# An audio tower on one core: coefficients, variances and head norms as rows spread by matmuls, expert gates spread by DMA, written-out orders for the whole run

## What is computed

```python
def _ssm_layer(x, A_log, Dp, W_dbc, W_dt, b_dt):
    A = -exp(A_log)
    delta, Bm, Cm = split(x @ W_dbc.T, [1, 1 + 64])          # one delta, 64 B, 64 C per token
    delta = softplus(delta @ W_dt.T + b_dt)
    hs = scan of h = exp(delta * A) * h + delta * x * Bm       # 64 states
    return sum over states of hs * Cm  + Dp * x
# three such layers; after the first two, pairs of steps are averaged (375 -> 187 -> 93)
h = tok(x)
h = h + attn(layernorm(h))     # q, k normalised per head of 8 channels; y divided by its own norm
h = h + moe(layernorm(h))      # router -> softmax -> top 2 of 6 experts; each 64-64-64-64 with relu
```

## Time and profile before

| | |
|---|---|
| median of 3 runs | 776.01 us (769.16 to 778.88) |
| the profiled execution, its own time | 778.98 us |
| its span in the trace | 777.2 us |
| mean granted TensorE clock | 0.952 |
| busy: PE, DVE, ACT, POOL | 87%, 79%, 67%, 43% |

### The profile page before, as it was taken

One profiled execution on the slowest core, in us unless ns is written; L12 is line 12 of the kernel. 1 busy time (PEld: TensorE's weight loads), 2 busy tenths in 40 slices (PEclk: granted clock), 3 DMA queues, 4 the chain that ended last, 5 costly groups with the idle time before them and its releaser, 6 DMA issues.

```text
span 777.2 us, 18707 instructions
## 1 busy us (share of the span) xinstructions
PE 677.7 (87%) x7686; PEld 317.6 (41%) x7686; DVE 617.4 (79%) x1082; ACT 524.6 (67%) x930; POOL 331.9 (43%) x291
## 2 busy tenths in 40 slices
PE   4766689899999999999999998999999997988774
PEld 2322234344444444444444453444444433433321
DVE  6899889789898989898989898987888986755230
ACT  1442476858788787878687968677786848575631
POOL 6455462636444646454645534353545252311000
PEclk9985899999999999999999999999999999999875
DMA  3332221112021211212030303111201001000001
GB/s 76 74 83 49 49 46 31 25 32 56 22 54 32 47 40 32 56 24 63 16 71 14 73 2 73 43 26 44 48 19 37 9 1 36 7 8 4 5 6 26
DMA packets 78694, 28.32 MB, mean 36 GB/s; under 512 B 70407, under 2 KB 78599, under 8 KB 78599
## 3 DMA queue, kind: packets, MB, share of 16 engines
q1 hardware_dynamic: 71904, 26.08, 14.7%
q10 hardware_dynamic: 6695, 0.95, 0.7%
HBM read 13.30 MB, written 3.05 MB: 21 GB/s over the span
## 4 chain that ended last, share of the span: by engine, by line
PE 65%; DVE 14%; ACT 11%; issue 4%; DMA 2%; SPq 2%; POOL 1%; DVEq 0%; ACTq 0%
PE ring L1004 19%; ACT pm L837 7%; PE ring L1074 6%; PE ring L1061 5%; PE ring L1160 4%; PE ring L1132 3%; PE ring L1011 3%; PE ring L1015 3%; PE ring L1036 3%; PE ring L1141 2%; PE ring L977 2%; PE ring L1123 2%; PE ring L1029 2%; PE ring L1098 2%; PE ring L1091 2%
## 5 line engine op out<-in xcount | busy, mean ns | idle before, releaser
L837 ACT ACTIVATE pm<-ring,two_col 93x744 f32<-93x744 f32 x128 | 105.8, 872 | 12.5 <-PE ring L1061 10.9
L1439 DVE TENSOR_TENSOR hidw<-hid,ring 128x744 f32<-128x744 f32 x48 | 44.4, 926 | 30.0 <-PE ring L1123 22.5
L1061 PE MATMUL ring<-q_exp,qk 32*93 32x372 f32 x512 | 56.4, 509 | 13.2 <-ACT pm L837 8.7
L1074 PE MATMUL ring<-pm,v 97*32 97x93 f32 x2048 | 53.5, 250 | 9.5 <-ACT pm L837 8.8
L693 POOL TENSOR_TENSOR h_in<-base_D,carry_D 128x372 f32<-128x372 f32 x16 | 17.0, 1061 | 102.2 <-DVE base_D L1327 102.2
L689 POOL TENSOR_TENSOR du_A<-delta_A,x_A 128x744 f32<-128x744 f32 x16 | 37.4, 2339 | 50.4 <-ACT delta_A L785 38.9
L872 ACT ACTIVATE hid<-ring,b_col 128x372 f32<-128x372 f32 x96 | 49.1, 563 | 8.2 <-PE ring L1141 8.2
L1074 PEld LDWEIGHTS ring<-pm,v 97*32 97x32 f32 x2048 | 42.3, 112 | 27.6 <-ACT pm L837 19.2
L711 POOL TENSOR_TENSOR q_exp<-qk,mask_q 128x1488 f32<-128x1488 f32 x16 | 42.9, 2682 | 17.6 <-DVE qk L1377 17.4
L879 ACT ACTIVATE hid<-ring,b_col 128x744 f32<-128x744 f32 x48 | 42.2, 878 | 12.0 <-PE ring L1132 7.9
L1132 PE MATMUL ring<-hid,w 64*64 64x372 f32 x384 | 42.8, 517 | 5.8 <-ACT v L829 3.4
(11 more groups left out here) (280 smaller groups left out, 1819.6 us busy)
## 6 DMA issues: line engine op xcount, KB each, us to landing
xin_A<-in_x_dram SPq DMA_DIRECT2D x62, 93.0 KB
xin_B<-in_x_dram SPq DMA_DIRECT2D x62, 93.0 KB
x_A<-x_A SPq DMA_DIRECT2D x32, 93.0 KB, 2.4
x_B<-x_B SPq DMA_DIRECT2D x32, 93.0 KB, 2.2
x_C<-x_C SPq DMA_DIRECT2D x32, 93.0 KB, 2.7
out_dram<-osb SPq DMA_DIRECT2D x15, 186.0 KB
x_D<-x_D SPq DMA_DIRECT2D x32, 46.5 KB, 1.9
w<-in_L_ffn_expert_w_dram SPq DMA_DIRECT2D x6, 48.0 KB
```

Source lines behind the costliest of these rows:

```text
L837: a.activation(pm[q % 2][h][0:TOUT].rearrange("m a j n -> m a (j n)"), out_of(f"att.s{q}{h}")[0:TOUT, :, 0:COLS], ACT.Square, bias=two_col ...
L1061: ins = mm(o[h][0:TOUT, b, 0:COLS], qk[r:r + 32, 1, q * TOUT:(q + 1) * TOUT], q_exp[r:r + 32, q].rearrange("p j n -> p (j n)"), start=True ...
L1074: ins = mm(o[32 * j:32 * j + 32, 0, h * TOUT:h * TOUT + TOUT], rows[:, at:at + 32], pm[q % 2][h][:, b, j, :], start=(b == 0), stop=(b == 1 ...
L1439: tt(hidw[k][:], hid2[:], out_of(f"ffn.g_{k}")[:, :, 0:COLS], ALU.mult).then_inc(me, 1)
```

## The change

- **Rows.** A new PE job `row` multiplies x with three weight columns into a few rows (128x32 weights, half or quarter of the columns), ACT copies them out (`rows`), and `dpre`, `b`, `c` become products of one-hot 64x64 blocks of ones (`row_back`) with these rows: eight matmuls of half the columns in place of four. W_dt becomes the scale of ACT's Exp. `alive` and the accumulators go; DVE takes the maximum of the rows instead (`most`), and at the end a few small steps make the flag.
- **Norms.** `cen` runs as four 64x64 blocks of 186 columns, `var` as four 128x32 ones of 93, ACT's Ln and Exp work on 93 columns in place of 372, and a new job `rs` spreads the result. The mean is taken out of the weights beforehand.
- **Head norms.** ACT evicts q and k with bias (`qkb`), squares them from SBUF, `n2` makes rows, clamp, Ln and Exp work on 186 columns, a new job `nq` spreads them, `hat` is one product. ACT copies v in place of DVE.
- **Gates.** The split, the selection matmuls and `hid2` go. PE transposes the gates in f32 to 6 partitions, ACT copies them, and a new step of SP, `gates`, copies each expert's partition to 64 partitions by DMA. `hidw` is one DVE operation, max(h2, -b2) times gate; what that leaves out is added to b3 beforehand.
- **Orders.** Every engine's list is written out for all 16 groups, and each PE job has a bank number of its own.

```diff
@@ SyncE @@
+                if s == "gates":
+                    need(g, "act ffn.gateT")
+                    need(g, *(f"dve ffn.hidw{k}" for k in range(NEP)), back=1)
+                    for e in range(NX):
+                        half = slice(E * (e % 2), E * (e % 2) + E)
+                        sp.dma_start(gate_all[half, e // 2].rearrange("p h c -> p (h c)"),
+                                     gateT[e:e + 1].rearrange("e h c -> e (h c)")[:, None, :].broadcast_to([1, E, 2 * COLS])).then_inc(done["sp ffn.gates"], 16)
@@ ScalarE @@
+                if s == "row":
...
+                    a.activation(rows[u][:], out_of(f"{u}.row", g)[:, 0, 0:WIDE[u] // 2], ACT.Copy).then_inc(me, 1)
...
-                    a.activation(rstd[w][:], rstd[w][:], ACT.Exp, scale=-0.5).then_inc(me, 1)
+                    a.activation(ln_rows[w][:], ln_rows[w][:], ACT.Exp, scale=-0.5).then_inc(me, 1)
...
+                        ins = a.activation(halves(qk_raw[:, b]), qk_made(b, g), ACT.Identity, bias=bqk_col[:, b:b + 1])
+                    ins.then_inc(me, 1)
+                if s == "qksq":
+                    need(g, "act att.qkb")
+                    need(g, "pe att.n2", back=1)
+                    a.activation(qk_sq[:], qk_raw[:], ACT.Square).then_inc(me, 1)
...
-                if s[:4] == "hid2":
...
-                    a.activation(hid2[:], out_of(f"ffn.h2_{k}")[:, :, 0:COLS], ACT.Relu, bias=b2_col[:, k:k + 1]).then_inc(me, 1)
...
+                    a.activation(gateT[:], out_of("ffn.gT", g)[0:NX, :, 0:COLS], ACT.Copy).then_inc(me, 1)
@@ TensorE @@
+                elif s == "row":
...
+                            ins = mm(o[to:to + 32, 0, 0:chunk], row_w[:, l].rearrange("p h r -> p (h r)"),
+                                     xs[u][:, b, h * chunk:(h + 1) * chunk], start=True, stop=True, tile_position=(0, to))
+                    ins.then_inc(me, 1)
+                elif s in ("dpre", "b", "c"):
+                    need(g, f"act {u}.row")
...
+                                ins = mm(o[to:to + E, b, h * chunk:(h + 1) * chunk], row_back[s][r:r + E, h, to:to + E],
+                                         rows[u][r:r + E, :], start=True, stop=True, tile_position=(r, to))
...
-                    mm(o[:, 0, 0:COLS], blk_mean[:], rstd[u[0]][:], start=True, stop=True).then_inc(me, 1)
+                    for q in range(NPAIR):
+                        ins = mm(o[32 * q:32 * q + 32, 0, 0:TOUT], ln_sum[:], cen_sq[u[0]][:, q * TOUT:(q + 1) * TOUT],
+                                 start=True, stop=True, tile_position=(0, 32 * q))
...
-                if s[:2] == "g_":
...
-                        ins = mm(o[:, h, 0:COLS], sel[:, h, k], gateT[:], start=True, stop=True)
...
+                            ins = nc.tensor.transpose(o[0:NX, h, q * TOUT:(q + 1) * TOUT], gate[:, 2 * q + h, :],
+                                                      ident[0:TOUT, 0:TOUT])
@@ VectorE @@
-                if s == "alive":
-                    need(g, f"act {u}.ln")
-                    v.tensor_reduce(seen[:, 0, FLAG[u], g:g + 1], delta[u][:], AX_X, ALU.min).then_inc(me, 1)
+                if s == "most":
+                    need(g, f"act {u}.row")
+                    v.tensor_reduce(seen[:, FLAG[u], g % NG:g % NG + 1], rows[u][:], AX_X, ALU.max).then_inc(me, 1)
...
-                    need(g, f"pe ffn.g_{k}", f"act ffn.hid2_{k}")
+                    need(g, f"pe ffn.h2_{k}", "sp ffn.gates")
                     need(g, "pe ffn.o", back=1)
-                    tt(hidw[k][:], hid2[:], out_of(f"ffn.g_{k}")[:, :, 0:COLS], ALU.mult).then_inc(me, 1)
+                    stt(hidw[k][:], out_of(f"ffn.h2_{k}", g)[:, :, 0:COLS], b2_neg[:, k:k + 1], gate_all[:, k],
+                        ALU.max, ALU.mult).then_inc(me, 1)
```

Of the orders the diff shows little:

```diff
-            "sp": ("D.swap:3 A.load:0 C.swap:2 B.load:0 ffn.store:7 A.swap:0 B.swap:0"),
...
+            "sp": ("prep.l1:0 prep.l4:0 prep.l0:0 A.load:0 A.load:1 A.swap:0 B.load:0 B.load:1 B.swap:0 A.load:2 "
...
+                    "D.swap:7 A.load:10 C.swap:8 ffn.gates:5 ffn.store:4 A.swap:9 B.load:11 B.swap:10 ffn.store:5 "
```

More of the change, by code:

```diff
@@ L96, in audio_tower @@
         m_quad = sb("m_quad", [P, LAYERS, P])
-        m_delta = sb("m_delta", [P, LAYERS, P])
-        m_b0 = sb("m_b0", [P, LAYERS, P])
-        m_c0 = sb("m_c0", [P, LAYERS, P])
+        row_w = sb("row_w", [P, LAYERS, 2, 16])
+        row_in = sb("row_in", [P, 16])
+        row_back = {j: sb(f"row_back_{j}", [P, 2, P]) for j in ("dpre", "b", "c")}
+        wdt_col = sb("wdt_col", [P, LAYERS])
+        nwdt_col = sb("nwdt_col", [P, LAYERS])
+        ones_row = sb("ones_row", [4, P])
+        most = sb("most", [P, 4])
+        most_of = sb("most_of", [4, 2])
+        most_at = sb("most_at", [4, 2, 4])
+        ends = sb("ends", [P, 2, 4])
+        least = sb("least", [P, 4])
         decay = sb("decay", [P, LAYERS, NS])
@@ L125, in audio_tower @@
         b2_col = sb("b2_col", [P, NEP])
[L126 to L127 removed]
+        b2_neg = sb("b2_neg", [P, NEP])
+        b2_at = sb("b2_at", [P, NEP, NX])
+        b3_row = sb("b3_row", [NX, E])
         def per_unit(name, extra=0):
@@ L141, in audio_tower @@
         carry = per_unit("carry")
-        base = per_unit("base")
-        seen = sb("seen", [P, 2, 4, NG])
+        base = quad
+        seen = sb("seen", [P, 4, NG])
+        rows = {u: sb(f"rows_{u}", [P, WIDE[u] // 2]) for u in UNITS}
         gen_w = sb("gen_w", [P, 2, P])
@@ L436, in audio_tower @@
         FFN_STEPS = NORM_STEPS + ["pe rh", "act rh", "pe lg", "dve route1", "act prexp", "dve top",
-                                  "act topexp", "dve gate", "pool split", "pe gT", "act gateT"]
+                                  "act topexp", "dve gate", "pe gT", "act gateT", "sp gates"]
         for k_ in range(NEP):
-            FFN_STEPS += [f"pe h1_{k_}", f"act hid1_{k_}", f"pe h2_{k_}", f"act hid2_{k_}", f"pe g_{k_}", f"dve hidw{k_}"]
+            FFN_STEPS += [f"pe h1_{k_}", f"act hid1_{k_}", f"pe h2_{k_}", f"dve hidw{k_}"]
         FFN_STEPS += ["pe o", "dve fin", "pe oT", "act out", "sp store"]
@@ L485, in audio_tower @@
         done = {who: sem(f"{who.replace(' ', '_').replace('.', '_')}_done") for who in
-                ("pe", "act", "dve", "pool", "sp A.load", "sp B.load", *(f"sp {u}.swap" for u in UNITS), "sp ffn.store")}
+                ("pe", "act", "dve", "pool", "sp A.load", "sp B.load", *(f"sp {u}.swap" for u in UNITS), "sp ffn.store", "sp ffn.gates")}
+        BANK = {(w, g): b for w, b in SPARE.items() for g in range(NG, 2 * NG)}
+        for entry in ORDER["pe"].split():
+            step_, banks_ = entry.split("/")
+            w_, g_ = step_.split(":")
+            BANK |= {(job, int(g_)): int(b) for job, b in zip(PAIRED.get(w_, (w_,)), banks_.split(","))}
         BEFORE = {}
@@ L902, in prepare @@
             def prepare(g, u, s):
+                if s == "ends":
+                    q = sem("ends_exp")
+                    need(g, "dve prep.ends")
+                    a.activation(least[:], least[:], ACT.Exp).then_inc(q, 1)
+                    act.wait_ge(q, 1)
+                    a.activation(least[:], least[:], ACT.Ln, bias=1.0).then_inc(me, 1)
                 for k in range(2):
@@ L945, in bank @@
                     need(g_e, *JOBS[earlier][1:])
-                return out_of(job)
+                return out_of(job, g)
             def prepare(g, u, s):
                 o = bank(g, f"prep.{s}")[:, 0]
+                if s == "most":
+                    need(g, "dve prep.most")
+                    nc.tensor.transpose(o[0:4, 0:P], most[:], ident[:]).then_inc(me, 1)
+                if s == "ends":
+                    need(g, "dve prep.mostof")
+                    mm(o[:, 0:8], ones_row[:], most_at[:].rearrange("p k u -> p (k u)"), start=True, stop=True).then_inc(me, 1)
                 if s == "flag":
@@ L1154, in experts @@
                     o = bank(g, "ffn.o")
-                    for i in range(3):
-                        mm(o[:, 0, 0:COLS], b3_part[i][:].rearrange("r h e -> r (h e)"), gateT[:],
-                           start=(i == 0), stop=(i == 2))
+                    for h in range(2):
+                        mm(o[E * h:E * h + E, 0, 0:COLS], b3_row[:], gateT[:, h], start=True, stop=False,
+                           skip_group_check=True, tile_position=(0, E * h))
                     for k in range(NEP):
@@ new lines, in prepare @@
+                if s == "ends":
+                    need(g, "pe prep.ends")
+                    found = out_of("prep.ends", g)[:, 0, 0:8].rearrange("p (k u) -> p k u", k=2)
+                    for u, l in UNITS.items():
+                        for k, w in enumerate((wdt_col, nwdt_col)):
+                            ts(ends[:, k, FLAG[u]:FLAG[u] + 1], found[:, k, FLAG[u]:FLAG[u] + 1], w[:, l:l + 1], bdt_col[:, l:l + 1],
+                               ALU.mult, ALU.add).then_inc(c, 1)
+                    dve.wait_ge(c, 8)
```

(7 more changed lines are left out.)

481 lines of the change are left out of this document (280 added, 201 removed), and 513 rows, old and new, of tables (FIRST, LAST, ORDER).

## The result

The changed kernel takes 1,379.2 us (median of 4 runs, 1,377.0 to 1,383.0), the kernel before 772.6 (767.2 to 778.9): a ratio of 1.790, 95% interval 1.776 to 1.804. It is slower by 607 us. The forecast was 1,250, and its own range, 930 to 1,400, holds the result; of the cases, the time is nearest to rival (c), 1,400.

A forecast was written before the change was run, and what follows sets the result against it. One source partition limits the gate DMAs, so DVE waits at `hidw`: 151 us to the first gate, 15 intervals of 68.8 (1,032), 44 for the last gates, 24 to the end: 1,251, about 1,250 us; own range 930 to 1,400, 8-in-10 range 740 to 1,400.

The forecast's parts named there:

- rival (c): Worse than forecast: PE at its lower clock in the stalls, swaps behind the gates late too; 1,400 us, chance 0.07.
- The gates' price: Six broadcast DMAs per group, each from one partition to 64, between `gate` and `hidw`: 41 us with landing.
- two engines' worth: Rate assumed for reading one source partition in the gate DMAs: 28.6 GB/s, 39 us before landing.
- us to landing of gate_all near 40: Sign in the changed kernel's profile: the gate DMAs' landing time on tile gate_all, near 40 us.
- DVE stands about 33 us per group: DVE, in order, waits at `hidw` for all six gate DMAs: about 33 us per group.
- The rows between: DVE's work before the next `gate` can come, priced by durations: 9 to 41 us per interval, mean 24.8.
- busy time within 15 us of before: Sign said to hold in either case: PE's busy time stays within 15 us of the kernel before.
- the one path: The path from `gate` to `hidw`, on which the prediction turns: intervals of 68.8 us in place of 39.9.
- Swap landings of tens of us: Sign on SP's queue: swaps stand behind the gate DMAs and take tens of us to land.
- The gains without the gates: Savings from the other parts: DVE 47 us, ACT 40 us, PE 0.65 us a group, start 10 us.
- case without the loss: Rival in which the broadcast is spread well and PE bounds again: 747 us, range 735 to 762, chance 0.25.
- rival (d): The new orders themselves lose a wait a group: 15 to 30 us; no chance given for it alone.

The follow-up runs named there:

- e12: Changed kernel with the six narrow gate DMAs issued from GpSimd's queue and `hidw` reading a constant tile without waiting for them: 1,257.4 us, ratio 1.617.
- e2: Changed kernel without the gate DMAs and the waits for them, gate_all holding the constant 0.25 from the start: 784.8 us, ratio 1.021.
- e7: Changed kernel, whole computation, with the gate written 16 times so that each gate DMA reads 16 partitions instead of one: 818.6 us, ratio 1.062.
- e6: Changed kernel with its narrow gate DMAs issued as before, but `hidw` reading a constant tile without waiting for them: 1,264.1 us, ratio 1.643.
- e11: Changed kernel, whole computation, `hidw` still waiting, with the six narrow gate DMAs moved from SyncE's queue to GpSimd's: 1,361.3 us, ratio 1.766.

## Why the prediction was right, and where not

**The gates' price: right, in size partly by luck.** The term "41 us with landing" measured 41.3 in the kernel and 41.8 alone. It stood on two engines' worth, 28.6 GB/s, chosen from a range of one to four (78 to 20 us); the choke gave 27 alone and 33 in e12 as a mean over the time in which its packets were held. No row before the change fixed that choice. The picture behind it was not quite what happened either: not two engines' streams pass, but sixteen engines are busy 86% of the time and move 27 GB/s together. The time of the six is the same by both, but only the second says that every other transfer is held as well. The sign "us to landing of gate_all near 40" did not come as written: one gate DMA lands in a median of 22.1 us, and 41 is the time of the six.

**DVE stands about 33 us per group: right.** 571.8 / 16 = 35.7 us. With the 3 us for transpose and copy, `gate` to `hidw` was summed as 44 and measured 45.8.

**The rows between, mis-sized.** The 24.8 us from `hidw` to the next `gate` measured 30.6. This is the largest term of the miss: 5.8 x 15 = 87 of the 127 us between 1,251 and the span of 1,378. It was priced from VectorE's durations alone, and its idle time was put at nothing. Summed in the trace, VectorE is busy 22.6 of the 30.6 us, 2.2 less than priced, and idle 8.0. In e2, where no gate DMA runs, it is busy the same 22.6 of 28.8 and idle 6.2: that much is VectorE's waiting for others in any case, and 1.8 us come with the gates. The rest of the miss: 1.8 x 15 = 27 in `gate` to `hidw`, 17 in the start, and 6 less at the end (62.4 against 68).

**Rival (c): both signs are there, but they explain little of the number.** The mean granted clock fell to 0.76 of full speed, between the levels of 1.2 and 2.4 GHz, and TensorE's busy time rose by 40 us over e2 with the same instructions; swaps landed late. The forecast of "busy time within 15 us of before" is wrong by that (33 more). But VectorE's path sets the interval, and from e7 to the changed kernel its part beside the gates grows by 1.3 us only (29.3 to 30.6). The time came out nearest to (c) for the reason above, not for (c)'s.

**What the prediction did not see** is that its wait was replaceable. It read the late swaps as a companion of the wait; e6 and e12 show that the same transfers hold the kernel at 1,260 with no wait at `hidw` at all. That this is also the forecast's number is chance, since the forecast got there by the wait. The steps of the sum held; its claim to be the one path did not.

**Swap landings of tens of us: half right.** Their median stays at 2.3 to 2.8 us; those that meet the gates take up to 14.8 us to land in the changed kernel, and the rest of their delay is that SyncE issues them late: at the wait of 38.8 us, the longest, 36.4 us lie before the issue of the swap.

**The gains without the gates: terms right, sum wrong.** `alive` went as said:

```profile
L1583 DVE TENSOR_REDUCE seen<-rows_A 128x1 f32<-128x186 f32 x16 | 5.4, 339 | 14.7 <-ACT rows_A L920 14.7
```

339 ns where it took 918, 32 us less over the units, and v's copy is gone. `hidw` cost 2 us, not 7. But `quad`'s three-operand steps cost 6 us more than `base`'s, and the router's rows up to `gate` 14 more, with no reason shown (8 and 12 in e2): VectorE has 30 us less in the changed kernel, not 47. ScalarE has 35 less, forecast 40. TensorE has 0.4 us a group less to do in e2 (6.6 us in all), forecast 0.65. For its case without the loss the prediction took 1.55 us off each interval; e2 shows 0.5. The start, forecast 10 us shorter, was 15 us longer. Together this turned 747 us into 785: 25 us in the start, 16 in the intervals, and 8 back at the end, which was to be 4 us longer and is 4 shorter (33 of the 38; the rest is the difference between a profiled execution and the median). By its kind this is rival (d), the orders, although the experiments do not show by which entries.

## What to carry to other kernels

Price a broadcast DMA at its narrower end: count the partitions that it reads as well as those that it writes, and if it reads one, write the row several times first (here 0.75 us of VectorE per group took 33.5 us off the way from `gate` to `hidw`). A slow transfer can cost more than its own wait: here every other transfer met the same engines, so before you hide the wait, ask what else needs a DMA in that time. And when one removal leaves the loss in place, remove two at once before you name the cause: here neither the wait nor the queue, nor both together, took away more than 122 of the 607 us, and the width of the source took away 561.

No version here beats the kernel before; the best with the whole computation is e7, at 1.062 of its time.

## What the runs showed of the hardware that was not expected

A gate DMA is issued in a median of 0.60 us in e7, and the first two of a group in 0.5 to 0.6 us in the changed kernel too, mostly; from the fourth on, with narrow ones ahead of it on SyncE's queue, it takes about 7 us. From GpSimd's queue the same six issue in 0.53 us each and land in a median of 27.4 us, but then issues on SyncE's queue are held: up to 20.3 us for a load of x and 27.7 for a swap in e12.

Sources of two and four partitions, each row repeated 32 and 16 times, were read at 24 and 37 GB/s with a DMA share of 0.12 and 0.20: few engines took part. One row repeated 64 times had a share of 0.86. Spreading a source over two partitions in this form was therefore no cure; sixteen was.

TensorE had idle time put to "issue", in which it waited for nothing that the profile shows: none in e2 and e7, 8.6 us in the changed kernel, 4.7 in e11, 49 in e6 and 153 in nine stalls of up to 26.7 us in e12. Instructions come in over DMA too (queue 8, 89 packets, 1.46 MB on each of these pages), and the packets' times in the traces settle what the stalls are: all twenty that last over 1 us, in the four runs, end 2.2 to 2.4 us after the start of a packet of queue 8. In e2 such a packet comes every 4 to 20 us; in e12 one starts at 620.4 us and the next at 663.1, with a group's gate DMAs under way from 623.2 to 665.2, and TensorE goes on at 665.5 after 26.7 us. So TensorE stood until its instructions had come, and their load was late. That the gate packets are what delayed the load is read from their coming together and from its absence in e2 and e7; no run moved only the one.
